# Cross-attention with group normalisation: whole-batch rounding and subtract, one chain of three GpSimd adds, and another order within a step

## The chip, the cores and the metric

The kernel runs on one core of one Trainium2 chip. The metric is the device time of one execution in microseconds (us). Engines are named as in the profile: PE is TensorE's matmul, PEld its weight load, DVE is VectorE, ACT is ScalarE, POOL is GpSimd, SP is SyncE, which issues the transfers of the loop.

## The reference

There are 32 batches. For each, `x` and `ctx` are 128 channels by 1024 positions, in float32.

```python
q = conv1x1(Wq, bq, ctx); k = conv1x1(Wk, bk, ctx); v = conv1x1(Wv, bv, x)   # 8 heads of 16 channels
scores = einsum('bhdl,bhel->bhde', q, k) / sqrt(128)       # channel by channel, within a head
attn = softmax(scores); out = einsum('bhde,bhel->bhdl', attn, v)
o = conv1x1(Wo, bo, out) + x
o_hat = (o - mean(o)) * rsqrt(var(o) + 1e-5)               # over all channels and positions of a batch
return o_hat * gn_w + gn_b
```

## The kernel before, in words

The scores need only the Gram matrix G = ctx·ctxᵀ (128x128) and the row sums s of ctx, and everything after the softmax is one matrix M with a bias, so that o = M·x. A batch thus goes through these pieces:

- **Gram.** ACT rounds ctx to a high part (`hl_sb[..., 0:C]`, line 340), DVE subtracts it from ctx to get the low part (`hl_sb[..., C:2C]`, line 432), PE multiplies the eight chunks into `g_ps` (`gram_products`, line 625). ACT copies the cross term (`b2_sb`, line 380), POOL adds up the low parts over the chunks (`lsuma`, `lsumb`, `lsum2`, `lsum`, lines 289 to 312), PE adds both into `g_ps`, and DVE writes `g_sb` and `s_sb` (lines 459, 460).
- **Scores.** PE makes `p_ps` from `g_sb` (`query_product`), DVE makes `p_sb` (line 477), PE makes `sc_ps` from `p_sb` and `sbk_sb` (lines 654, 655), DVE adds the mask and takes the smallest value of a row (`sc_sb`, `smin`, line 423).
- **Softmax and M.** ACT takes the exponential (line 335), DVE the reciprocal of the sums (`zinv`, line 443), ACT scales (line 352), PE multiplies (`softmax_product`), ACT copies (`r_sb`, line 363), PE makes `m_ps` in two products, DVE writes `m_sb` (`folded_matrix`, line 409).
- **Output.** PE makes `o_ps` in two halves of 512 columns (`products_of_x`), DVE takes statistics of each half (`bn`, lines 465 and 471), then `mv` and `mrow` (lines 502, 504). PE averages `mrow` over the channels (`mean`), DVE makes `dev` and `vrow` (lines 414, 416), PE averages `vrow` (`variance`), DVE makes `veps` (line 447), POOL makes `nshift`, `wshift` and `rstd` (lines 272 to 281), DVE makes `gain` and `shift` (lines 451, 453), and ACT writes the normalised batch to `out_sb` (line 371).

All matmuls are called through one helper, so all have line 535 in the trace and are told apart by their tiles.

The kernel is a software pipeline over the batches, written by hand. In step t every engine runs one fixed list of instructions, in which batch t is rounded, t-1 goes through the Gram products, t-2 through the scores, t-3 through softmax and M, t-4 through the output products and statistics, and t-5 is normalised. Each engine runs its list in order, step after step; engines are held together by semaphores alone, and an instruction whose semaphore isn't there holds up all that stands behind it on its engine. The two lists that matter most here are these, in a step of the kernel before:

- DVE: `dev`, `vrow` (batch t-5); `sc_sb`, `smin` (t-3); low part of the second half of ctx (t-1); `zinv`; `veps`; `g_sb`, `s_sb` (t-2); `bn` of the first half of o (t-4); `gain`, `shift` (t-5); `bn` of the second half; `p_sb`; `mv`, `mrow`; `m_sb`; low part of the first half of ctx (batch t).
- PE: first half of o; `variance`; the two additions into `g_ps`; second half of o; `query_product`; `softmax_product`; six Gram chunks; the two products of M; two Gram chunks; `mean`; the two products of `sc_ps`.

The lines on which the order rests:

```python
if has(t, 2):                     # PE, near the middle of its step
    query_product()               # waits for g_copied, which DVE's g_sb gives
...
    product(sc_ps, p_sb[:, :], wkT, stop=False)          # PE, the end of its step
    product(sc_ps, wqT[:, :], sbk_sb[:, :], start=False).then_inc(sc_ready, 1)
...
    dve.wait_ge(sc_ready, done)   # DVE, before sc_sb
```

Of the kernel before, what the change touches and what calls it, by code (L numbers as in the profile page):

```python
# [21 lines left out]
def xattn_groupnorm_kernel(nc, x, yT, weights, biases, columns, out):  # L22
# [27 lines left out]
    with ExitStack() as ctx:  # L50
# [338 lines left out]
        def _(dve):  # L389
            nc.vector.memset(onesn[:, :], 1.0 / E).then_inc(const_dve, 1)  # L390
# [10 lines left out]
            def step(t0, k):  # L401
# [9 lines left out]
                if has(t, 5):  # L411

                    dve.wait_ge(mu_ready, t - 4)
                    nc.vector.tensor_tensor(dev[:, h1:h1 + 1], mrow[:, h1:h1 + 1], mu_ps, ALU.subtract).then_inc(dev_ready, 1)  # L414
                    dve.wait_ge(dev_ready, t - 4)
                    nc.vector.tensor_scalar(vrow[:, h1:h1 + 1], dev[:, h1:h1 + 1], dev[:, h1:h1 + 1], mv[:, h1, 1:2],  # L416
                                            ALU.mult, ALU.add).then_inc(vrow_ready, 1)
# [9 lines left out]
                def rest_half(b, half):  # L427

                    ky = (k + b) % UNROLL
                    chunks = slice(half * HCH, (half + 1) * HCH)  # L430
                    dve.wait_ge(h_ready, (t + b) * 2 + 1 + half)
                    nc.vector.tensor_tensor(hl_sb[:, ky, chunks, C:2 * C], y_sb[:, ky, chunks, :],  # L432
                                            hl_sb[:, ky, chunks, 0:C].bitcast(F32), ALU.subtract).then_inc(l_ready, 1)
# [11 lines left out]
                def variance():  # L445
                    dve.wait_ge(var_ready, t - 4)
                    nc.vector.tensor_scalar(veps[:, h1:h1 + 1], var_ps, EPS, None, ALU.add).then_inc(veps_ready, 1)  # L447

                def affine():
                    dve.wait_ge(rstd_ready, t - 4)  # L450
                    nc.vector.tensor_scalar(gain[:, h1:h1 + 1], gn_w, rstd[:, h1:h1 + 1], None, ALU.mult)  # L451
                    dve.wait_ge(wshift_ready, t - 4)
                    nc.vector.tensor_scalar(shift[:, h1:h1 + 1], wshift[:, h1:h1 + 1], rstd[:, h1:h1 + 1], gn_b,  # L453
                                            ALU.mult, ALU.add).then_inc(affine_ready, 1)

                def gram():
# [4 lines left out]

                def statistics():

                    dve.wait_ge(o_ready, (t - 4) * 2 + 1)
                    nc.vector.bn_stats(bn[:, h, 0, :], o_ps[:, h, 0:HALF])  # L465
                    if has(t, 5) and not is_step(t, RUSH + 1):
                        affine()
                    if is_step(t, RUSH):
                        folded_matrix()
# [224 lines left out]
```

## Time and profile before

| | |
|---|---|
| time, median of 3 runs | 190.53 us (190.33 to 190.54) |
| the profiled execution: its own time | 190.41 us |
| its span, first to last instruction | 188.4 us |
| busy PE, DVE | 171.4 us, 162.1 us |
| busy ACT, POOL | 125.5 us, 125.7 us |
| mean granted TensorE clock | 0.968 of full |
| moved between HBM and the core | 50.8 MB, mean 270 GB/s |

Busy time of PE is modelled for overlapping matmuls and does not mean that it can go no faster. The 2.0 us between the profiled execution's time and its span lie before the first and after the last instruction. `sc_sb` is a good mark of a step, since it runs once in each from step 3 to step 34.

### The profile page before, as it was taken

The numbers are of one execution on the slowest core, as the hardware profiler recorded it, in microseconds if no ns is written. First come the engines' busy times: TensorE is split into PE (matmuls) and PEld (weight loads), VectorE is DVE, ScalarE is ACT, GpSimd is POOL, SyncE is SP. The second block draws the span as 40 slices with busy tenths as digits, with TensorE's granted clock in tenths as the row PEclk, the third lists the DMA queues.
The fourth block names the chain that finished last, engine by engine and source line by source line (L and its number), as shares of the span: only waits on it lengthen the run. The fifth ranks groups of instructions, "written<-read, shape, count | busy, mean of one in ns | idle before, by whom it ended". The sixth has DMA issues, their size and how long they took to land.

```text
span 188.4 us, 4194 instructions
## 1 busy us (share of the span) xinstructions
PE 171.4 (91%) x996; PEld 129.2 (69%) x996; DVE 162.1 (86%) x586; ACT 125.5 (67%) x290; POOL 125.7 (67%) x234
## 2 busy tenths in 40 slices
PE   7877999999999999999999999999999999998830
PEld 7767776767777777777677767776777767775420
DVE  1833899999899989998999989998999899977552
ACT  4433577787677877777777767876777777765321
POOL 3773577777777788877777777778777777762030
PEclk9985999999999999999999999999999999999995
DMA  6799377888878888888899787889888865622305
GB/s 211 264 418 381 94 277 250 322 325 320 310 284 296 303 288 297 317 303 318 304 324 342 291 289 273 317 296 305 291 313 315 321 229 223 221 100 88 148 23 203
DMA packets 14408, 50.82 MB, mean 270 GB/s; under 512 B 1728, under 2 KB 1856, under 8 KB 14400
## 3 DMA queue, kind: packets, MB, share of 16 engines
q1 hardware_dynamic: 13968, 50.34, 73.2%
q10 hardware_dynamic: 432, 0.40, 0.8%
q8 instruction: 3, 0.05, 0.1%
q14 instruction: 5, 0.04, 0.1%
HBM read 33.95 MB, written 16.78 MB: 269 GB/s over the span
## 4 chain that ended last, share of the span: by engine, by line
DVE 58%; issue 12%; POOL 7%; PE 6%; ACT 1%; POOLq 1%; DVEq 0%
DVE hl_sb L432 17%; DVE bn L471 10%; DVE bn L465 7%; POOL lsuma L312 4%; DVE mv L502 3%; DVE m_sb L409 3%; PE ps_ps L535 2%; DVE sc_sb L423 2%; DVE g_sb L459 2%; POOL rstd L281 2%; DVE shift L453 2%; DVE mrow L504 2%; PE st_ps L535 2%; DVE zinv L443 2%; DVE gain L451 2%
## 5 line engine op out<-in xcount | busy, mean ns | idle before, releaser
L535 PE MATMUL o_ps<-x_sb,m_sb 128*128 128x512 f32 x128 | 68.6, 618 | 0.4 <-DVE m_sb L409 0.4
L432 DVE TENSOR_TENSOR hl_sb<-y_sb,hl_sb 128x512 fp32r<-128x512 f32 x64 | 55.2, 863 | 2.3 <-ACT hl_sb L340 2.1
L535 PE MATMUL g_ps<-hl_sb 128*128 128x258 f32 x256 | 47.2, 308 | 0.0
L371 ACT ACTIVATE out_sb<-o_ps,shift,gain 128x1024 f32<-128x1024 f32 (+1 forms) x32 | 38.1, 1191 | 8.0 <-DVE shift L453 7.8
L340 ACT CAST hl_sb<-y_sb 128x512 fp32r<-128x512 f32 x64 | 39.1, 615 | 3.9 <-DMA y_sb<-in_ctx_dram 3.9
L304 POOL TENSOR_TENSOR lsum<-lsum 128x128 fp32r<-128x128 f32 x32 | 15.2, 474 | 33.1 <-DVE hl_sb L432 25.3
L535 PEld LDWEIGHTS g_ps<-hl_sb 128*128 128x128 f32 x256 | 35.7, 195 | 0.1
L312 POOL TENSOR_TENSOR lsuma<-hl_sb 128x256 f32<-128x256 f32 x32 | 27.4, 856 | 3.1 <-DVE hl_sb L432 3.1
L335 ACT ACTIVATE a_sb<-sc_sb,smin 128x128 f32<-128x128 f32 x32 | 12.9, 402 | 21.7 <-DVE smin L423 21.7
L296 POOL TENSOR_TENSOR lsum<-lsuma,lsumb 128x256 f32<-128x256 f32 x32 | 23.4, 730 | 4.3
L289 POOL TENSOR_TENSOR lsumb<-hl_sb 128x256 f32<-128x256 f32 x32 | 24.0, 750 | 1.4 <-DVE hl_sb L432 1.4
L535 PEld LDWEIGHTS ps_ps<-wqT,g_sb 128*128 128x128 f32 x64 | 10.4, 192 | 20.0 <-DVE g_sb L459 13.5
L535 PEld LDWEIGHTS st_ps<-vrow,onesn 128*128 128x128 f32 x64 | 12.0, 190 | 15.2 <-DVE vrow L416 8.0
L465 DVE BATCH_NORM_STATS2 bn<-o_ps 128x6 f32<-128x512 f32 x32 | 21.9, 685 | 0.2 <-PE o_ps L535 0.2
L471 DVE BATCH_NORM_STATS2 bn<-o_ps 128x6 f32<-128x512 f32 x32 | 21.9, 684 | 0.0
L272 POOL TENSOR_TENSOR nshift<-dev,mv 128x1 f32<-128x1 f32 x32 | 15.5, 483 | 8.7 <-DVE dev L414 8.7
L535 PEld LDWEIGHTS o_ps<-x_sb,m_sb 128*128 128x128 f32 x128 | 19.4, 192 | 0.8 <-DVE m_sb L409 0.5
L281 POOL TENSOR_TENSOR rstd<-veps,nhalf 128x1 f32<-128x1 f32 x32 | 17.5, 548 | 3.2 <-DVE veps L447 3.2
L535 PEld LDWEIGHTS st_ps<-mrow,onesn 128*128 128x128 f32 x64 | 9.5, 188 | 12.5 <-DVE mrow L504 12.5
L535 PE MATMUL st_ps<-mrow,onesn 128*128 128x1 f32 x64 | 12.1, 259 | 5.7 <-DVE mrow L504 4.6
L363 ACT COPY r_sb<-rm_ps 128x128 f32<-128x128 f32 x32 | 8.5, 266 | 12.8 <-PE rm_ps L535 12.8
L352 ACT ACTIVATE a_sb<-a_sb,zinv 128x128 f32<-128x128 f32 x32 | 12.8, 400 | 5.3 <-DVE zinv L443 5.2
(58 smaller groups left out, 315.3 us busy)
## 6 DMA issues: line engine op xcount, KB each, us to landing
y_sb<-in_ctx_dram SPq DMA_DIRECT2D x32, 512.0 KB, 3.9
x_sb<-in_x_dram SPq DMA_DIRECT2D x32, 512.0 KB, 4.9
out_dram<-out_sb SPq DMA_DIRECT2D x31, 512.0 KB, 3.9
out_dram<-out_sb SPq DMA_DIRECT2D x2, 256.0 KB, 2.2
w_in<-in_weights_dram ACTq DMA_DIRECT2D x1, 256.0 KB, 8.9
rows<-in_biases_dram ACTq DMA_DIRECT2D x1, 128.0 KB, 6.4
cols<-in_columns_dram ACTq DMA_DIRECT2D x1, 3.0 KB, 3.4
```

The costliest lines, as they stand in the source:

```text
L272: nc.gpsimd.tensor_tensor(nshift[:, h1:h1 + 1], dev[:, h1:h1 + 1], mv[:, h1, 0:1], ALU.subtract).then_inc(nshift_ready, 1)
L281: nc.gpsimd.tensor_tensor(rstd[:, h1:h1 + 1], veps[:, h1:h1 + 1], nhalf[:, :], ALU.pow).then_inc(rstd_ready, 1)
L289: nc.gpsimd.tensor_tensor(lsumb[:, :, :], low[:, 0:HCH // 2, :], low[:, HCH // 2:HCH, :], ALU.add).then_inc(lsumb_ready, 1)
L296: nc.gpsimd.tensor_tensor(lsum2[:, :, :], lsuma[:, :, :], lsumb[:, :, :], ALU.add).then_inc(lsum2_ready, 1)
L304: nc.gpsimd.tensor_tensor(lsum[:, h1, :], lsum2[:, 0, :], lsum2[:, 1, :], ALU.add).then_inc(lsum_ready, 1)
L312: nc.gpsimd.tensor_tensor(lsuma[:, :, :], low[:, 0:HCH // 2, :], low[:, HCH // 2:HCH, :], ALU.add).then_inc(lsuma_ready, 1)
L340: nc.scalar.copy(hl_sb[:, k, chunks, 0:C], y_sb[:, k, chunks, :]).then_inc(h_ready, 1)
L371: nc.scalar.activation(out_sb[:, ko, part], o_ps[:, h1, part], ACT.Identity, bias=shift[:, h1:h1 + 1], scale=gain[:, h1:h1 + 1]).then_inc( ...
L432: nc.vector.tensor_tensor(hl_sb[:, ky, chunks, C:2 * C], y_sb[:, ky, chunks, :], hl_sb[:, ky, chunks, 0:C].bitcast(F32), ALU.subtract).the ...
L465: nc.vector.bn_stats(bn[:, h, 0, :], o_ps[:, h, 0:HALF])
L471: nc.vector.bn_stats(bn[:, h, 1, :], o_ps[:, h, HALF:L]).then_inc(bn_done, 1)
L535: return nc.tensor.matmul(dst, lhsT, rhs, start=start, stop=stop, **more)
```

## The change

- **Rounding and subtract.** ACT rounds a whole batch of ctx (128x1024) at once, in the place of the first half; DVE makes the low part of the whole batch t-1 at once, right behind `sc_sb`. The semaphores count one per batch instead of two.
- **GpSimd.** The four adds of a batch (two of 256 columns from `hl_sb`, one of 256, one of 128) become three: `lsum4` (512 columns), `lsum2` (256), `lsum` (128). `nshift` and `wshift` leave GpSimd, and `rstd` stays, now first in its step.
- **Mean and variance.** `onesn` holds -1/128. PE's `mean` stands between the products of M and the last two Gram chunks. DVE's `dev` and `vrow` run at the end of the same step instead of at the start of the next, and between them stands a new instruction that makes `wshift` there.
- **Gain and shift.** Both move from DVE to ACT, behind the scaling by `zinv` and ahead of `sbk_sb` and `r_sb`.
- **DVE's order.** In a step it is now: `sc_sb`, `smin`; low part of the whole batch t-1; `zinv`; `veps`; `bn` of the first half; `g_sb`, `s_sb`; `bn` of the second half; `mv`, `mrow`; `p_sb`; `m_sb`; `dev`, `wshift`, `vrow`. PE's list is otherwise as before.

The first steps and the last three have the same moves, with the exceptions for `RUSH` (step 34) simplified: in step 35 the mean no longer stands behind the first half of o.

```diff
 POOL
-                    pool.wait_ge(dev_ready, t - 4)
-                    nc.gpsimd.tensor_tensor(nshift[:, h1:h1 + 1], dev[:, h1:h1 + 1], mv[:, h1, 0:1],
-                                            ALU.subtract).then_inc(nshift_ready, 1)
...
-                    nc.gpsimd.tensor_tensor(wshift[:, h1:h1 + 1], nshift[:, h1:h1 + 1], gn_w,
-                                            ALU.mult).then_inc(wshift_ready, 1)
                     pool.wait_ge(veps_ready, t - 4)
                     nc.gpsimd.tensor_tensor(rstd[:, h1:h1 + 1], veps[:, h1:h1 + 1], nhalf[:, :], ALU.pow).then_inc(rstd_ready, 1)
...
-                    nc.gpsimd.tensor_tensor(lsumb[:, :, :], low[:, 0:HCH // 2, :], low[:, HCH // 2:HCH, :],
-                                            ALU.add).then_inc(lsumb_ready, 1)
+                    nc.gpsimd.tensor_tensor(lsum4[:, :, :], low[:, 0:HCH, :], low[:, HCH:CH, :],
+                                            ALU.add).then_inc(lsum4_ready, 1)
...
-                if has(t, 0):
...
-                    nc.gpsimd.tensor_tensor(lsuma[:, :, :], low[:, 0:HCH // 2, :], low[:, HCH // 2:HCH, :],
-                                            ALU.add).then_inc(lsuma_ready, 1)
 ACT
-                    round_half(0)
+                    nc.scalar.copy(hl_sb[:, k, :, 0:C], y_sb[:, k, :, :]).then_inc(h_ready, 1)
                 if has(t, 3):
                     act.wait_ge(zinv_ready, t - 2)
                     nc.scalar.mul(a_sb[:, :], a_sb[:, :], zinv[:, h1:h1 + 1]).then_inc(a_ready, 1)
+                if has(t, 5):
+                    act.wait_ge(rstd_ready, t - 4)
+                    nc.scalar.mul(gain[:, h1:h1 + 1], gn_w, rstd[:, h1:h1 + 1])
+                    nc.scalar.activation(shift[:, h1:h1 + 1], wshift[:, h1:h1 + 1], ACT.Identity,
+                                         bias=gn_b, scale=rstd[:, h1:h1 + 1]).then_inc(affine_ready, 1)
 DVE
-                if has(t, 1):
-                    rest_half(-1, 1)
+                if has(t, 1):
+                    ky = (k - 1) % UNROLL
+                    dve.wait_ge(h_ready, t)
+                    nc.vector.tensor_tensor(hl_sb[:, ky, :, C:2 * C], y_sb[:, ky, :, :],
+                                            hl_sb[:, ky, :, 0:C].bitcast(F32), ALU.subtract).then_inc(l_ready, 1)
...
-                if has(t, 2):
-                    gram()
-                if has(t, 4):
-                    statistics()
+                if has(t, 4):
+                    dve.wait_ge(o_ready, (t - 4) * 2 + 1)
+                    nc.vector.bn_stats(bn[:, h, 0, :], o_ps[:, h, 0:HALF])
...
+                if has(t, 2):
                     dve.wait_ge(g_ready, t - 1)
                     nc.vector.tensor_tensor(g_sb[:, :], g_ps[:, 0:C], b2_sb[:, :].bitcast(F32), ALU.add).then_inc(g_copied, 1)
                     nc.vector.tensor_copy(s_sb[:, :], s_ps).then_inc(s_copied, 1)
...
-                if has(t, 0):
-                    rest_half(0, 0)
+                if has(t, 4):
+                    dve.wait_ge(mu_ready, t - 3)
+                    nc.vector.tensor_tensor(dev[:, h:h + 1], mrow[:, h:h + 1], mu_ps, ALU.add).then_inc(dev_ready, 1)
...
+                    nc.vector.scalar_tensor_tensor(out=wshift[:, h:h + 1], in0=mu_ps, scalar=m_sb[:, h, E:E + 1],
+                                                   in1=gn_w, op0=ALU.add, op1=ALU.mult)
+                    dve.wait_ge(dev_ready, t - 3)
+                    nc.vector.tensor_scalar(vrow[:, h:h + 1], dev[:, h:h + 1], dev[:, h:h + 1], mv[:, h, 1:2],
+                                            ALU.mult, ALU.add).then_inc(vrow_ready, 1)
 PE
                     product(m_ps[:, E:E + 1], r_sb[:, :], bv).then_inc(m_ready, 1)
+                if has(t, 4):
+                    mean()
                 if has(t, 1):
                     gram_products(range(GRAM_BEFORE_M, CH)).then_inc(hl_ready, 1)
...
-                if has(t, 4) and not is_step(t, RUSH):
-                    mean(-4)
```

## Rows read from the trace of the kernel before

**Rows 1.** The page: busy time by engine, and the chain that ended last.

```profile
PE 171.4 (91%) x996; PEld 129.2 (69%) x996; DVE 162.1 (86%) x586; ACT 125.5 (67%) x290; POOL 125.7 (67%) x234
...
DVE 58%; issue 12%; POOL 7%; PE 6%; ACT 1%; POOLq 1%; DVEq 0%
```

**Rows 2.** Timeline, one steady step: start, duration, engine, instruction, [idle before, releaser].

```profile
96.87 0.29 DVE L423 CUSTOM_DVE_ANT_0 sc_sb<-ps_ps,k 128x128 f32<-128x128 f32 x1
...
97.03 0.73 POOL L312 TENSOR_TENSOR lsuma<-hl_sb 128x256 f32<-128x256 f32 x1
...
97.17 1.14 DVE L432 TENSOR_TENSOR hl_sb<-y_sb,hl_sb 128x512 fp32r<-128x512 f32 x1
...
98.23 0.15 DVE L443 RECIPROCAL zinv<-zsum 128x1 f32<-128x1 f32 x1
...
98.36 0.28 DVE L459 TENSOR_TENSOR g_sb<-g_ps,b_sb 128x128 f32<-128x128 f32 x1
...
98.57 0.55 POOL L281 TENSOR_TENSOR rstd<-veps,nhalf 128x1 f32<-128x1 f32 x1
98.62 0.69 DVE L465 BATCH_NORM_STATS2 bn<-o_ps 128x6 f32<-128x512 f32 x1
98.69 0.30 PEld L535 LDWEIGHTS ps_ps<-wqT,g_sb 128*128 128x128 f32 x2 [0.63 <-DVE g_sb L459]
...
99.01 0.39 PE L535 MATMUL rm_ps<-w_in,a_sb 128*128 128x128 f32 x2
...
99.22 0.19 DVE L451 TENSOR_SCALAR gain<-cols,rstd 128x1 f32<-128x1 f32 x1
...
99.44 0.27 ACT L363 COPY r_sb<-rm_ps 128x128 f32<-128x128 f32 x1 [0.30 <-PE rm_ps L535]
...
100.33 0.49 PE L535 MATMUL g_ps<-hl_sb 128*128 128x258 f32 x2
...
100.87 0.30 PEld L535 LDWEIGHTS st_ps<-mrow,onesn 128*128 128x128 f32 x2 [0.27 <-DVE mrow L504]
...
101.42 0.39 PE L535 MATMUL ps_ps<-sbk_sb,wqT 128*128 128x128 f32 x2
...
101.96 0.29 DVE L423 CUSTOM_DVE_ANT_0 sc_sb<-ps_ps,k 128x128 f32<-128x128 f32 x1
```

**Rows 3.** Timeline of DVE in every fourth step, where the subtract meets no GpSimd add.

```profile
86.50 0.29 DVE L423 CUSTOM_DVE_ANT_0 sc_sb<-ps_ps,k 128x128 f32<-128x128 f32 x1
...
86.72 0.69 DVE L432 TENSOR_TENSOR hl_sb<-y_sb,hl_sb 128x512 fp32r<-128x512 f32 x1
87.36 0.16 DVE L443 RECIPROCAL zinv<-zsum 128x1 f32<-128x1 f32 x1
```

**Rows 4.** Timeline of PE in an early step, where the mean came without a wait.

```profile
23.36 0.49 PE L535 MATMUL g_ps<-hl_sb 128*128 128x258 f32 x2
...
24.14 0.39 PE L535 MATMUL ps_ps<-sbk_sb,wqT 128*128 128x128 f32 x2
```

**Rows 5.** Groups by line and shape, GpSimd's adds: busy us, mean ns, idle before.

```profile
L289 POOL TENSOR_TENSOR lsumb<-hl_sb 128x256 f32<-128x256 f32 x32 | 24.0, 750 | 1.4 <-DVE hl_sb L432 1.4
...
L304 POOL TENSOR_TENSOR lsum<-lsum 128x128 fp32r<-128x128 f32 x32 | 15.2, 474 | 33.1 <-DVE hl_sb L432 25.3 <-issue 7.6
```

**Rows 6.** Timelines: `sc_sb` of steps 3, 4, 6 and 33.

```profile
14.21 0.29 DVE L423 CUSTOM_DVE_ANT_0 sc_sb<-ps_ps,k 128x128 f32<-128x128 f32 x1 [1.09 <-PE ps_ps L535]
...
20.03 0.29 DVE L423 CUSTOM_DVE_ANT_0 sc_sb<-ps_ps,k 128x128 f32<-128x128 f32 x1 [0.46 <-PE ps_ps L535]
...
29.91 0.29 DVE L423 CUSTOM_DVE_ANT_0 sc_sb<-ps_ps,k 128x128 f32<-128x128 f32 x1
...
168.72 0.29 DVE L423 CUSTOM_DVE_ANT_0 sc_sb<-ps_ps,k 128x128 f32<-128x128 f32 x1 [0.20 <-PE ps_ps L535]
```

**Rows 7.** Windows of the start: busy PE, PEld, DVE, ACT, POOL, then clock, DMA share, GB/s.

```profile
9.40:14.10 4.70, 3.33 (x21) 3.17 (x21) 1.81 (x6) 1.80 (x4) 3.32 (x6) 0.85 1.03 418
14.10:18.80 4.70, 3.50 (x17) 3.41 (x17) 1.75 (x8) 1.86 (x6) 1.76 (x3) 0.50 1.01 383
```

More of the change, by code:

```diff
@@ L285, in step @@
-                    pool.wait_ge(l_ready, t * 2)
+                    low = hl_sb[:, (k - 1) % UNROLL, :, C:2 * C].bitcast(F32)
+                    pool.wait_ge(l_ready, t)
                     if exists(t, 2):
                         pool.wait_ge(lsum2_ready, t - 1)
-                    nc.gpsimd.tensor_tensor(lsumb[:, :, :], low[:, 0:HCH // 2, :], low[:, HCH // 2:HCH, :],
-                                            ALU.add).then_inc(lsumb_ready, 1)
-                    pool.wait_ge(lsuma_ready, t)
@@ L380, in step @@
                     nc.scalar.copy(b2_sb[:, :], g_ps[:, C:2 * C]).then_inc(b2_copied, 1)
-                if has(t, 0) and not ahead:
-                    round_half(1)
             pipeline(act, step, first=3 * UNROLL)
@@ L409, in folded_matrix @@
                     nc.vector.tensor_tensor(m_sb[:, h1, :], m_ps, ident[:, :], ALU.add).then_inc(m_copied, 1)
[L411 to L417, printed above, removed]
                 if has(t, 3):
@@ L425, in step, with variance @@
                                                    accum_out=smin[:, h1:h1 + 1]).then_inc(smin_ready, 1)
[L427 to L433, printed above, removed]
+                def variance():
+                    dve.wait_ge(var_ready, t - 4)
+                    nc.vector.tensor_scalar(veps[:, h1:h1 + 1], var_ps, -1.0, EPS, ALU.mult, ALU.add).then_inc(veps_ready, 1)
+                if has(t, 5) and is_step(t, RUSH):
+                    variance()
                 if has(t, 1):
-                    rest_half(-1, 1)
+                    ky = (k - 1) % UNROLL
+                    dve.wait_ge(h_ready, t)
+                    nc.vector.tensor_tensor(hl_sb[:, ky, :, C:2 * C], y_sb[:, ky, :, :],
+                                            hl_sb[:, ky, :, 0:C].bitcast(F32), ALU.subtract).then_inc(l_ready, 1)
                 if is_step(t, 2):
@@ L440, in step @@
                     nc.vector.tensor_scalar(wqT[:, :], w_in[:, 0, :], -SCALE, None, ALU.mult).then_inc(const_dve, 1)
-                def inverse_sums():
+                if has(t, 3):
                     dve.wait_ge(exp_done, t - 2)
                     nc.vector.reciprocal(zinv[:, h1:h1 + 1], zsum[:, h1:h1 + 1]).then_inc(zinv_ready, 1)
[L445 to L456, printed above, removed]
+                if has(t, 5) and not is_step(t, RUSH) and not is_step(t, RUSH + 1):
+                    variance()
+                if has(t, 4):
+                    dve.wait_ge(o_ready, (t - 4) * 2 + 1)
+                    nc.vector.bn_stats(bn[:, h, 0, :], o_ps[:, h, 0:HALF])
+                if is_step(t, RUSH + 1):
+                    variance()
+                if has(t, 2):
                     dve.wait_ge(g_ready, t - 1)
@@ L460, in gram @@
                     nc.vector.tensor_copy(s_sb[:, :], s_ps).then_inc(s_copied, 1)
[L462 to L469, printed above, removed]
+                if is_step(t, RUSH):
+                    folded_matrix()
+                if has(t, 4):
+                    done = value(t - 3)
                     dve.wait_ge(o_ready, (t - 3) * 2)
                     nc.vector.bn_stats(bn[:, h, 1, :], o_ps[:, h, HALF:L]).then_inc(bn_done, 1)
[L473 to L499 removed]
                     dve.wait_ge(c_loaded, 16 * N_CONST)
@@ L579, in softmax_product, with mean @@
                     product(r_ps, a_sb[:, :], woT).then_inc(r_ready, 1)
-                def mean(b):
-                    pe.wait_ge(mrow_ready, t + b + 1)
-                    if exists(t, 1 - b):
-                        pe.wait_ge(veps_ready, t + b)
-                    row = (h + b) % 2
-                    product(mu_ps, onesn[:, :], mrow[:, row:row + 1]).then_inc(mu_ready, 1)
+                def mean():
+                    pe.wait_ge(mrow_ready, t - 3)
+                    if exists(t, 5):
+                        pe.wait_ge(veps_ready, t - 4)
+                    product(mu_ps, onesn[:, :], mrow[:, h:h + 1]).then_inc(mu_ready, 1)
                 if has(t, 5) and is_step(t, RUSH):
@@ L598, in step @@
                     products_of_x(0)
-                if is_step(t, RUSH + 1):
-                    mean(-5)
-                elif has(t, 5) and not is_step(t, RUSH):
+                if has(t, 5) and not is_step(t, RUSH):
                     variance()
@@ L643, in step @@
                     product(m_ps[:, E:E + 1], r_sb[:, :], bv).then_inc(m_ready, 1)
+                if has(t, 4):
+                    mean()
                 if has(t, 1):
```

67 lines of the change are left out of this document (16 added, 51 removed).

## The prediction

> **What bounds the kernel now.** I read the page first: DVE and PE are both near full, and the chain that ended last runs mostly on DVE [rows 1]. That suggests that a microsecond taken from DVE is a microsecond won. It is only half the story, so I looked next at the timeline of one steady step, side by side for DVE and PE [rows 2], and followed who hands what to whom. Each engine works its list in order, and two hand-overs join the lists into a ring. `sc_sb`, the first of the big instructions of DVE's step, starts 0.15 us after PE's last product of the step before ends (101.42 + 0.39 = 101.81, against 101.96). And PE's `query_product` can't load before DVE's `g_sb` ends (98.64; the load starts at 98.69, after an idle weight port released by `g_sb`). Everything that PE does from there to its `sc_ps` products stands in order behind `query_product`. So a step can't be shorter than DVE's stretch from `sc_sb` to the end of `g_sb` (98.64 - 96.87 = 1.77), plus PE's stretch from there to the end of `sc_ps` (101.81 - 98.64 = 3.17), plus 0.15: together 5.09, which is exactly the distance of the two `sc_sb` in rows 2. Within PE's stretch lies a wait of 0.27 for `mrow`, which is DVE work behind `g_sb`. The ring and DVE's own load are thus both tight: DVE is without a real pause, and what DVE has after `g_sb` reaches PE through `mrow`.
>
> Over the whole run the step is a little longer: 27 steps from `sc_sb` at 29.91 to the one at 168.72 [rows 6] take 138.81, or 5.14 each.
>
> **The change part by part, for a steady step.** I place it against `sc_sb` = 0.
>
> DVE up to `g_sb`. The low part is now one subtract of 1024 columns. In the kernel before, the subtract of 512 in this place took 1.14, because it met POOL's add (97.03 to 97.76, [rows 2]): what is left after 97.76 is 0.55, the time of 512 columns. Where it met none it took 0.69, started 0.22 after `sc_sb` and gave way to `zinv` 0.64 later [rows 3]. The extra 512 columns cost 0.53 (a `bn` of 512 columns against 128 columns of `g_sb`: (0.69 - 0.28)/384 = 1.07 ns a column, 0.55 for 512; 0.60 with a start of its own). I take 0.53, so `zinv` starts at 0.22 + 0.64 + 0.53 = 1.39, against 1.36 before (98.23 - 96.87). So the bigger subtract costs nothing in this stretch, *if* POOL is idle during it. It is: POOL's chain starts behind `rstd`, about 1.70 to 2.25; an add of 512 columns is (750 - 474)/128 = 2.16 ns a column, so 0.75 + 0.55 = 1.30; then 0.75 and 0.47 [rows 5]; with gaps it ends at about 5.0, and the next subtract starts at 5.6.
>
> From `zinv` to `g_sb` were 0.13 us (98.23 to 98.36). Now `bn` of the first half stands between: its slot is 0.60 (98.62 to 99.22). Its data are long there. So `g_sb` starts at 1.39 + 0.13 + 0.60 = 2.12 and ends at 2.40, where it was 1.77. That is +0.63 on the ring.
>
> The Trainium skill ("SBUF — State Buffer", section "SBUF: two separate sides") says that the port pair that VectorE and GpSimd share is an exclusive lock, held for a whole instruction by a VectorE instruction with two SBUF inputs or by GpSimd. The trace agrees: 1.14 against 0.69 [rows 2, 3]. By that rule alone the change looks like a gain on VectorE of some 0.45 us a step, for the subtract then meets nobody.
>
> PE from `g_sb` to `sc_ps`. The weight load follows 0.05 after `g_sb`; 0.32 later `softmax_product` runs (98.69 to 99.01); 1.32 later come the last two Gram chunks (99.01 to 100.33). From there to the end of `sc_ps` with a mean that did not wait: 24.14 + 0.39 - 23.36 = 1.17 [rows 4], against 1.48 before. The mean's new place, two products earlier, doesn't change the sum, and it will not wait: DVE has `mrow` done at about 3.6, PE reaches the mean at 4.1. PE's stretch is 0.05 + 0.32 + 1.32 + 1.17 = 2.86, where it was 3.17: -0.31, the wait for `mrow` that goes.
>
> The step: 2.40 + 2.86 + 0.15 = **5.41**. PE now stands idle about 0.6 before `query_product`; DVE stands idle before `sc_sb`.
>
> What DVE saves buys nothing. It loses the collision (0.45), one start of a subtract (0.06), and `gain` and `shift` (99.22 to about 99.52, 0.30), and gains `wshift` (not in the trace; between 0.06 and 0.25, the slots of one-column and of 128-column instructions; I take 0.12). That brings it from 5.09 to about 4.4. All of it lies behind `g_sb` or, for the subtract, is used up ahead of it. Its end: `m_sb` waits for PE's second product of M (about 4.2), `dev` for the mean (4.5), and `vrow` ends near 5.0, 0.4 before the next `sc_sb`; so those waits stay off the ring.
>
> ACT. The round of 1024 columns follows the exponential and ends at about 1.9, half a step before it is needed by the next step. `gain` waits for `rstd` (ready at 2.3: `veps` at 1.46, then 0.55 on POOL [rows 2]). `gain`, `shift` and `sbk_sb` then end at about 3.1. Behind them is `r_sb`, whose product is ready at 3.2; PE wants it after six Gram chunks, at 3.8, and it takes 0.27 [rows 2]. So ACT's insertion costs nothing, with 0.3 of cover. The output instruction of 1.2 us ends near 4.7 and PE wants its buffer at 5.1.
>
> Transfers. SP's load of ctx waits for the whole low part, as it did for the second half, at the same place; at 5.41 us a step the demand falls. Cost 0.
>
> **The sum.** 27 steps from step 6 to 33: 27 x 5.41 = 146.1 against 138.8: +7.3. Steps 4 to 6 (20.03 to 29.91, 9.88 for two): 10.82, +0.9. Step 3 to 4: no `bn` yet, but the whole subtract stands before `g_sb`: +0.5. The first Gram matrix waits for the weights' transfer either way: 0. Step 33 has no subtract, and its mean no longer waits: -0.3. The tail: in step 34 the mean of batch 30 stands ahead of the first half of o of batch 31 (+1.3 on PE), but DVE no longer makes `gain` and `shift` before `mv` of batch 31; I find +0.1. Sum +8.5. On the profiled execution's own 190.41 this is 198.9; the median of the runs, 190.53, gives 199.0.
>
> **Rivals.**
> 1. *DVE alone is the bound* (for: 58% of the chain and no pause [rows 1]). Then its savings count, and PE's load, at most 5.09 - 0.27 = 4.82, is the next bound: (4.82 - 5.14) x 29 = -9, so **181**. Against it: `query_product` waits for `g_sb` by the code, and the row shows that wait. It decides if PE's stretch were 0.3 shorter than I read. 0.07. A ring that comes out at 5.14, no change: 0.03; a ring just below, 186 to 190: 0.03.
> 2. *ACT becomes part of the ring.* If `rstd` comes over 0.3 later than 2.3 or ACT's one-column instructions are as long as the 128-column ones, `r_sb` comes late for M, at 0.1 to 0.3 a step: **202 to 207**. A collision of POOL's chain with the subtract (if it ends after 5.6) would give as much. 0.12.
> 3. *The granted clock.* At the start it fell to 0.50, which is the 1.2 GHz level, after a stretch in which PE was busy for 3.33 of 4.70 us [rows 7]. PE will be busy for 4.8 of 5.4 in the steady steps, so I expect full clock there. But step 3 gets another 0.5 of idleness; if the low clock lasts one step longer, PE's 4.8 us of work in it takes up to twice as long: +2 to +4, **201 to 203**. 0.10. The Trainium skill ("TensorE: Matmul & The Clock Gate", section "What's actually happening") says that the throttled state is the default and activity releases it, which is what rows 7 show in small.
> 4. The forecast itself, 196 to 201.5: 0.65.
>
> The range: the terms unsure by about 0.1 a step give 2.8 either way; with the lower part of rivals 2 and 3 it is 195.5 to 203.5. A difference under 0.2% can't be told from none here. Faster 0.09, same 0.03, slower 0.88.
>
> **What would show it.** `sc_sb` every 5.4 us; the subtract at 1.2 us with POOL idle; `zinv` 1.4 after `sc_sb` and `g_sb` 2.1 after it; PE's weight load for `query_product` idle by about 0.6, released by `g_sb`; no wait for `mrow` before the mean; DVE waiting on PE before `sc_sb`, for some 0.4 a step, and its busy share down to about 80%. I am wrong if PE's wait before `query_product` is near zero, or if a step shows a new wait for `r_sb` or `rstd`.

## The result, and the profile after

The changed kernel takes 197.92 us (median of 4 runs, 196.82 to 199.13); the kernel before took 190.43 beside it. The ratio is 1.0405, with a 95% interval of 1.0331 to 1.0479: slower, by about 4%. The forecast was 199.0. Ratios, here and below, are of the executions in the faster of two states alone; the medians are of all.

The page of the changed kernel, busy time by engine and the chain that ended last, answers to [rows 1]:

```profile
PE 169.0 (86%) x996; PEld 125.8 (64%) x996; DVE 145.6 (74%) x522; ACT 137.5 (70%) x322; POOL 98.2 (50%) x138
...
PE 39%; DVE 27%; issue 19%; POOL 6%; DMA 5%; DVEq 1%; POOLq 1%; ACT 0%; ACTq 0%
```

DVE has lost 16.5 us of work and POOL 27.5, and the span grew from 188.4 to 195.6. No engine is above 86% of the span. In the steady part, 28.2 to 170 us, PE was busy for 131.01 of 141.80 us (92%, before 98%) and DVE for 116.31 (82%, before 96%). So neither is full any more; the time is set by who waits for whom, and the chain runs back and forth between PE and DVE. The list of waits names the pair (waiting instruction <- what it waited for: us in total, times, longest):

```profile
PEld ps_ps L479 <- DVE g_sb L419: 30.7, 25, 1.7
...
DVE sc_sb L384 <- PE ps_ps L479: 15.0, 32, 1.3
...
PE ps_ps L479 <- DVE g_sb L419: 14.5, 31, 1.6
...
ACT gain L326 <- POOL rstd L267: 11.3, 31, 4.1
```

In the step shown below the weight load (PEld) stands idle for 1.23 us before `query_product` and the matmuls for 0.40; in [rows 2] the weight load had 0.63 and the matmuls no wait. So the row of the matmuls tells better what PE lost.

Timeline of the changed kernel, one steady step, to be laid beside [rows 2]:

```profile
100.60 0.29 DVE L384 CUSTOM_DVE_ANT_0 sc_sb<-ps_ps,k 128x128 f32<-128x128 f32 x1 [0.43 <-PE ps_ps L479]
...
100.82 1.22 DVE L398 TENSOR_TENSOR hl_sb<-y_sb,hl_sb 128x1024 fp32r<-128x1024 f32 x1
...
101.96 0.15 DVE L407 RECIPROCAL zinv<-zsum 128x1 f32<-128x1 f32 x1
...
102.09 0.69 DVE L413 BATCH_NORM_STATS2 bn<-o_ps 128x6 f32<-128x512 f32 x1
...
102.69 0.27 DVE L419 TENSOR_TENSOR g_sb<-g_ps,b_sb 128x128 f32<-128x128 f32 x1
...
102.77 1.28 POOL L275 TENSOR_TENSOR lsum<-hl_sb 128x512 f32<-128x512 f32 x1
102.83 0.29 ACT L326 ACTIVATE gain<-cols,rstd 128x1 f32<-128x1 f32 x1 [0.16 <-POOL rstd L267]
...
103.02 0.49 PE L479 MATMUL ps_ps<-wqT,g_sb 128*128 128x128 f32 x2 [0.40 <-DVE g_sb L419]
...
103.34 0.39 PE L479 MATMUL rm_ps<-w_in,a_sb 128*128 128x128 f32 x2
...
103.77 0.27 ACT L339 COPY r_sb<-rm_ps 128x128 f32<-128x128 f32 x1
...
103.99 0.21 DVE L432 TENSOR_SCALAR mrow<-mv,m_sb 128x1 f32<-128x1 f32 x1
...
104.18 0.31 PEld L479 LDWEIGHTS rm_ps<-r_sb,w_in 128*128 128x128 f32 x2
...
104.63 0.30 PEld L479 LDWEIGHTS st_ps<-mrow,onesn 128*128 128x128 f32 x2
...
104.83 0.29 DVE L377 TENSOR_TENSOR m_sb<-rm_ps,ident 128x129 f32<-128x129 f32 x1 [0.38 <-PE rm_ps L479]
...
104.88 0.48 PE L479 MATMUL g_ps<-hl_sb 128*128 128x258 f32 x2
...
105.42 0.39 PE L479 MATMUL ps_ps<-sbk_sb,wqT 128*128 128x128 f32 x2
...
105.95 0.29 DVE L384 CUSTOM_DVE_ANT_0 sc_sb<-ps_ps,k 128x128 f32<-128x128 f32 x1 [0.43 <-PE ps_ps L479]
```

Read it as a ring. From `sc_sb` to the end of `g_sb` are 102.96 - 100.60 = 2.36 us; from there to the end of PE's `sc_ps` 105.81 - 102.96 = 2.85; then 0.14 to the next `sc_sb`: 5.35 in all. The subtract of 1024 columns lets `zinv` start 1.36 after `sc_sb`, as it was before with 512 columns and a collision. All the growth of the first stretch is the 0.60 of `bn`, which now stands between `veps` and `g_sb`. The weight load of `mean` (104.63) shows no wait, as `mrow` had ended at 104.20; before it had 0.27. Both engines of the ring now have pauses, DVE 0.43 before `sc_sb` (and 0.38 before `m_sb`), PE 0.40 before `query_product`.

`sc_sb` of steps 4, 6 and 33 in the changed kernel, which answer to [rows 6]:

```profile
20.16 0.29 DVE L384 CUSTOM_DVE_ANT_0 sc_sb<-ps_ps,k 128x128 f32<-128x128 f32 x1 [1.31 <-PE ps_ps L479]
...
30.80 0.29 DVE L384 CUSTOM_DVE_ANT_0 sc_sb<-ps_ps,k 128x128 f32<-128x128 f32 x1 [0.43 <-PE ps_ps L479]
...
175.76 0.29 DVE L384 CUSTOM_DVE_ANT_0 sc_sb<-ps_ps,k 128x128 f32<-128x128 f32 x1 [0.44 <-PE ps_ps L479]
```

The 27 steps between the last two take 144.96, or 5.37 each (three of 5.35 and one of 5.43 for each turn of the loop), against 138.81 before. That is +6.15 of the +7.2 by which the span grew. Steps 4 to 6 give +0.76, step 3 to 4 +0.33, step 33 to 34 -0.18, the tail +0.34, and the start up to step 3 -0.20.

### The profile page after: what moved, and what is told of

Same layout as the page of the kernel before. It is cut to its first block, busy times and chain, and to the rows that moved or that the text cites. A ratio compares the mean times of both kernels' runs of the same rounds, so it can differ in the third digit from the quotient of the medians.

```text
span 195.6 us, 3989 instructions
## 1 busy us (share of the span) xinstructions
PE 169.0 (86%) x996; PEld 125.8 (64%) x996; DVE 145.6 (74%) x522; ACT 137.5 (70%) x322; POOL 98.2 (50%) x138
## 4 chain that ended last, share of the span: by engine, by line
PE 39%; DVE 27%; issue 19%; POOL 6%; DMA 5%; DVEq 1%; POOLq 1%; ACT 0%; ACTq 0%
PE g_ps L479 15%; PE ps_ps L479 13%; DVE hl_sb L398 10%; DVE bn L413 8%; PE rm_ps L479 8%; DMA w_in<-in_weights_dram 5%; PE st_ps L479 3%; DVE g_sb L419 3%; DVE sc_sb L384 3%; POOL lsum L275 3%; DVE zinv L407 2%; POOL lsum L281 1%; POOL rstd L267 1%; POOL lsum L287 1%; DVE veps L390 1%
## 5 line engine op out<-in xcount | busy, mean ns | idle before, releaser
L275 POOL TENSOR_TENSOR lsum<-hl_sb 128x512 f32<-128x512 f32 x32 | 40.9, 1278 | 10.3 <-DVE hl_sb L398 10.3
L398 DVE TENSOR_TENSOR hl_sb<-y_sb,hl_sb 128x1024 fp32r<-128x1024 f32 x32 | 39.1, 1221 | 2.6 <-ACT hl_sb L318 2.6
L318 ACT CAST hl_sb<-y_sb 128x1024 fp32r<-128x1024 f32 x32 | 33.1, 1033 | 3.8 <-DMA y_sb<-in_ctx_dram 3.8
L479 PEld LDWEIGHTS ps_ps<-wqT,g_sb 128*128 128x128 f32 x64 | 9.5, 188 | 39.5 <-DVE g_sb L419 30.7
L479 PE MATMUL ps_ps<-wqT,g_sb 128*128 128x128 f32 x64 | 15.6, 325 | 14.5 <-DVE g_sb L419 14.5
L281 POOL TENSOR_TENSOR lsum<-lsum 128x256 f32<-128x256 f32 x32 | 23.4, 732 | 2.5
L384 DVE CUSTOM_DVE_ANT_0 sc_sb<-ps_ps,k 128x128 f32<-128x128 f32 x32 | 9.3, 292 | 15.0 <-PE ps_ps L479 15.0
L377 DVE TENSOR_TENSOR m_sb<-rm_ps,ident 128x129 f32<-128x129 f32 x32 | 9.4, 294 | 14.6 <-PE rm_ps L479 14.5
L352 ACT CAST b_sb<-g_ps 128x128 fp32r<-128x128 f32 x32 | 8.5, 266 | 13.3 <-PE g_ps L479 13.3
L326 ACT ACTIVATE gain<-cols,rstd 128x1 f32<-128x1 f32 x32 | 9.4, 295 | 11.3 <-POOL rstd L267 11.3
```

What stands on the lines that cost most here:

```text
L275: nc.gpsimd.tensor_tensor(lsum4[:, :, :], low[:, 0:HCH, :], low[:, HCH:CH, :], ALU.add).then_inc(lsum4_ready, 1)
L281: nc.gpsimd.tensor_tensor(lsum2[:, :, :], lsum4[:, 0:HCH // 2, :], lsum4[:, HCH // 2:HCH, :], ALU.add).then_inc(lsum2_ready, 1)
L318: nc.scalar.copy(hl_sb[:, k, :, 0:C], y_sb[:, k, :, :]).then_inc(h_ready, 1)
L384: nc.vector.tensor_tensor_reduce(out=sc_sb[:, :], in0=sc_ps, in1=k0[:, :], scale=1.0, scalar=3e38, op0=ALU.add, op1=ALU.min, accum_out=smi ...
L398: nc.vector.tensor_tensor(hl_sb[:, ky, :, C:2 * C], y_sb[:, ky, :, :], hl_sb[:, ky, :, 0:C].bitcast(F32), ALU.subtract).then_inc(l_ready, 1)
L479: return nc.tensor.matmul(dst, lhsT, rhs, start=start, stop=stop, **more)
```

## The experiments

The measure I trust most is the step, (`sc_sb` of step 33 less that of step 6)/27 in the profile, because executions of one kernel differ at their start. Times are medians; ratios are to the kernel before, measured beside each.

| kernel | step, us | time, us | ratio (95%) |
|---|---|---|---|
| before | 5.14 | 190.53 | |
| changed | 5.37 | 197.92 | 1.0405 (1.0331 to 1.0479) |
| 1 changed, `g_sb` first | 5.10 | 190.29 | 0.9993 (0.9934 to 1.0052) |
| 2 before, first `bn` ahead of `g_sb` | 5.39 | 196.39 | 1.0377 (1.0292 to 1.0461) |
| 3 changed, `gain` and `shift` on DVE | 5.37 | 199.58 | 1.0540 (1.0451 to 1.0629) |
| 4 changed, 0.33 us more ahead of `g_sb` | 5.70 | 208.37 | 1.0972 (1.0873 to 1.1071) |
| 5 changed, the same at the step's end | 5.37 | 197.82 | 1.056 (1.0479 to 1.0641) |
| 6 as 1, `sbk_sb` ahead of `gain` | 4.97 | 186.57 | none |
| 7 as 6, `mean` behind the Gram chunks | 4.87 | 183.69 | 0.9744 (0.9692 to 0.9795) |
| 8 as 1, `gain`/`shift` on DVE, `mean` late | 5.08 | 189.30 | 1.0046 (1.0015 to 1.0077) |
| 9 changed, idle products in step 3 | 5.37 | 196.67 | 1.0415 (1.0373 to 1.0457) |
| 10 as 7, idle products in step 3 | 4.87 | 182.30 | 0.9639 (0.9586 to 0.9691) |
| 11 as 7, again | 4.87 | 182.96 | 0.9655 (0.9601 to 0.9709) |

**1. Undo the one move in the changed kernel.**

```diff
 DVE, changed kernel
+                if has(t, 2):
+                    dve.wait_ge(g_ready, t - 1)
+                    nc.vector.tensor_tensor(g_sb[:, :], g_ps[:, 0:C], b2_sb[:, :].bitcast(F32), ALU.add).then_inc(g_copied, 1)
+                    nc.vector.tensor_copy(s_sb[:, :], s_ps).then_inc(s_copied, 1)
                 if has(t, 4):
                     dve.wait_ge(o_ready, (t - 4) * 2 + 1)
                     nc.vector.bn_stats(bn[:, h, 0, :], o_ps[:, h, 0:HALF])
-                if has(t, 2):
-                    dve.wait_ge(g_ready, t - 1)
-                    nc.vector.tensor_tensor(g_sb[:, :], g_ps[:, 0:C], b2_sb[:, :].bitcast(F32), ALU.add).then_inc(g_copied, 1)
-                    nc.vector.tensor_copy(s_sb[:, :], s_ps).then_inc(s_copied, 1)
```

> The changed kernel with g_sb and s_sb ahead of the first bn on DVE, nothing else. Theory (the ring sc_sb, g_sb, query_product, sc_ps sets the step): g_sb ends at about 1.76 us after sc_sb instead of 2.36, so the wait of PE before query_product goes. PE then comes early enough to wait for mrow (done 3.60 after sc_sb, mean reached at about 3.4): a step of about 4.95 instead of 5.37, time 185 to 187. Rival (the cause is ACT's gain and shift, or the whole-batch subtract): the place of one statistics instruction among DVE's changes nothing, the time stays at 197 to 199.

The step fell to 5.10 and the time to that of the kernel before. So the place of `g_sb` was the loss, but the gain was 0.27 a step where I expected 0.42, and the time stayed above the expected 185 to 187. The timeline of this kernel shows why:

```profile
92.39 0.28 DVE L413 TENSOR_TENSOR g_sb<-g_ps,b_sb 128x128 f32<-128x128 f32 x1
...
93.14 0.30 ACT L326 ACTIVATE gain<-cols,rstd 128x1 f32<-128x1 f32 x1 [0.16 <-POOL rstd L267]
...
93.33 0.37 ACT L327 ACTIVATE shift<-wshift,cols,rstd 128x1 f32<-128x1 f32 x1
...
93.61 0.39 ACT L335 ACTIVATE sbk_sb<-rows,s_sb 128x128 f32<-128x128 f32 x1
93.91 0.24 ACT L339 COPY r_sb<-rm_ps 128x128 f32<-128x128 f32 x1
...
94.20 0.30 PEld L479 LDWEIGHTS rm_ps<-r_sb,w_in 128*128 128x128 f32 x2 [0.17 <-ACT r_sb L339]
```

`g_sb` is ready 0.60 sooner (its end comes 1.76 after `sc_sb`, against 2.36), and PE now arrives at the products of M before `r_sb` is there. ACT copies `r_sb` only after `gain`, `shift` and `sbk_sb`, and `gain` waits for POOL's `rstd`. This was rival 2 of the prediction, hidden in the changed kernel by the later `g_sb`. Run 6 tests it.

**2. Do the one move alone, in the kernel before.**

```diff
 DVE, kernel before
                 def statistics():
-                    dve.wait_ge(o_ready, (t - 4) * 2 + 1)
-                    nc.vector.bn_stats(bn[:, h, 0, :], o_ps[:, h, 0:HALF])
...
+                if has(t, 4):
+                    dve.wait_ge(o_ready, (t - 4) * 2 + 1)
+                    nc.vector.bn_stats(bn[:, h, 0, :], o_ps[:, h, 0:HALF])
                 if has(t, 2):
                     gram()
```

> The kernel before with only this of the change: the first bn ahead of g_sb and s_sb on DVE. Theory: the ring grows by the 0.60 us of bn and loses the wait for mrow of 0.27, so a step of about 5.42 instead of 5.14 and a time of 197 to 200: this one move gives the whole loss. Rival: the loss comes from the other parts of the change, and the time stays within 1 us of 190.5.

The step is 5.39, and the time 196.39, a little below the expected 197 to 200. In the step this one move costs as much as the whole change (+0.25 against +0.23), and in the time nearly as much. The rest of the change, on which DVE and POOL save 44 us of busy time, shows no gain beside it (5.37 against 5.39). A small part of this kernel's step is DVE's own list: in three of four steady steps `sc_sb` starts 0.20 after PE's `sc_ps` ends, where it is 0.14 in the changed kernel. PE's wait appears in this kernel's timeline too, though DVE has all its old work:

```profile
101.27 0.27 DVE L459 TENSOR_TENSOR g_sb<-g_ps,b_sb 128x128 f32<-128x128 f32 x1
...
101.59 0.49 PE L536 MATMUL ps_ps<-wqT,g_sb 128*128 128x128 f32 x2 [0.51 <-DVE g_sb L459]
...
103.41 0.29 DVE L409 TENSOR_TENSOR m_sb<-rm_ps,ident 128x129 f32<-128x129 f32 x1 [0.28 <-PE rm_ps L536]
```

**3. Take back ACT's part.** `gain` and `shift` go back to DVE, between the second `bn` and `mv`.

```diff
 ACT
-                if has(t, 5):
-                    act.wait_ge(rstd_ready, t - 4)
-                    nc.scalar.mul(gain[:, h1:h1 + 1], gn_w, rstd[:, h1:h1 + 1])
-                    nc.scalar.activation(shift[:, h1:h1 + 1], wshift[:, h1:h1 + 1], ACT.Identity,
-                                         bias=gn_b, scale=rstd[:, h1:h1 + 1]).then_inc(affine_ready, 1)
 DVE
                     nc.vector.bn_stats(bn[:, h, 1, :], o_ps[:, h, HALF:L]).then_inc(bn_done, 1)
+                if has(t, 5):
+                    dve.wait_ge(rstd_ready, t - 4)
+                    nc.vector.tensor_scalar(gain[:, h1:h1 + 1], gn_w, rstd[:, h1:h1 + 1], None, ALU.mult)
+                    nc.vector.tensor_scalar(shift[:, h1:h1 + 1], wshift[:, h1:h1 + 1], rstd[:, h1:h1 + 1], gn_b,
+                                            ALU.mult, ALU.add).then_inc(affine_ready, 1)
+                if has(t, 4):
```

> The changed kernel with gain and shift back on DVE, behind the second bn. Theory: 0.30 us more on DVE lies behind g_sb and inside its idle time, and ACT's load of two instructions was covered: no change in the step (5.37), time 197 to 199. Rival (ACT's two instructions hold up r_sb or the output): the step falls by 0.1 to 0.3, time 189 to 195. Rival (DVE's load is what counts): plus 0.3 a step, 206.

The step is 5.37, unchanged: two instructions on either engine are off the ring, as the theory says. The time is 0.6 us above the expected range. In the profile the surplus over the changed kernel lies outside the steps: `sc_sb` of step 6 comes at 32.24 instead of 30.80, and the tail behind `sc_sb` of step 34 is 16.1 instead of 15.3. The start had the low clock for longer (0.50 and 0.58 between 14.1 and 23.5 us, where the changed kernel had 0.76 and 0.88). Whether this edit has a part in that is not settled.

**4 and 5. The same cost in two places.** One more statistics instruction of 256 columns a step, which nobody reads.

```diff
 DVE, run 4
                     nc.vector.bn_stats(bn[:, h, 0, :], o_ps[:, h, 0:HALF])
+                    nc.vector.bn_stats(extra[:, :], o_ps[:, h, 0:HALF // 2])
```

```diff
 DVE, run 5
                                             ALU.mult, ALU.add).then_inc(vrow_ready, 1)
+                    nc.vector.bn_stats(extra[:, :], o_ps[:, h, 0:HALF // 2])
```

> The changed kernel with one more statistics instruction of 256 columns a step on DVE, between the first bn and g_sb; nobody reads what it writes. Its slot is about 0.33 us. Theory: all of it lands on the ring, 30 x 0.33 = 10 us, time 207 to 209. Rival (DVE has 25% idle and PE is the bound): less than 2 us.

> The changed kernel with the same additional statistics instruction of 256 columns (0.33 us), now at the end of DVE's step, behind vrow. Theory: DVE waits there for PE anyway, 0.43 us before each sc_sb, so the instruction is hidden: step 5.37, time as the changed kernel within 1.5 us (196 to 199.5). Rival (any DVE work costs): 207.

Ahead of `g_sb` it lengthens each step from 5.37 to 5.70: all of its 0.33 slot (103.37 to 103.70 in that kernel's timeline), and PE's wait before `query_product` grows by the same, from 0.40 to 0.73. At the end of the step it costs nothing, 5.37. Its timeline shows it in what was the wait for `sc_ps`:

```profile
104.37 0.27 DVE L453 TENSOR_SCALAR vrow<-dev,mv 128x1 f32<-128x1 f32 x1
104.55 0.42 DVE L455 BATCH_NORM_STATS2 extra<-o_ps 128x6 f32<-128x256 f32 x1
105.07 0.29 DVE L385 CUSTOM_DVE_ANT_0 sc_sb<-ps_ps,k 128x128 f32<-128x128 f32 x1
```

This is the cleanest reading of the case: the same instruction on the same engine costs everything or nothing, by where it stands. (The ratio of run 5 is high because the kernel before was faster beside it, 188.36; the step, which repeats within 0.01, shows no cost.)

**6. Free `r_sb` in the order of run 1.**

```diff
 ACT, on top of run 1
+                if has(t, 2):
+                    if is_step(t, 2):
+                        act.wait_ge(c_loaded, 16 * N_CONST)
+                    act.wait_ge(s_copied, t - 1)
+                    nc.scalar.mul(sbk_sb[:, :], bkB, s_sb[:, :]).then_inc(sbk_ready, 1)
                 if has(t, 5):
                     act.wait_ge(rstd_ready, t - 4)
...
-                if has(t, 2):
-                    if is_step(t, 2):
-                        act.wait_ge(c_loaded, 16 * N_CONST)
-                    act.wait_ge(s_copied, t - 1)
-                    nc.scalar.mul(sbk_sb[:, :], bkB, s_sb[:, :]).then_inc(sbk_ready, 1)
```

> The changed kernel with g_sb ahead of the first bn and, on ACT, sbk_sb ahead of gain and shift. With g_sb first alone the step came to 5.10 instead of 4.95, because PE waited 0.17 us for r_sb, which stood behind rstd, gain, shift and sbk_sb on ACT. Theory: with sbk_sb in ACT's wait for rstd, r_sb comes 0.24 us sooner and the wait goes; the step falls to 4.93 to 4.97, time 184.5 to 187. Rival (r_sb was not what held it): 5.10, 189 to 190.

`sbk_sb` now fills ACT's wait for `rstd`, PE no longer waits for `r_sb`, and the step is 4.97, as expected. No ratio could be taken for it (its seven executions spread from 183.30 to 188.52), and the reading rests on the step.

**7. Put `mean` back.**

```diff
 PE, on top of run 6
-                if has(t, 4):
-                    mean()
                 if has(t, 1):
                     gram_products(range(GRAM_BEFORE_M, CH)).then_inc(hl_ready, 1)
...
+                if has(t, 4):
+                    mean()
```

> As the run with sbk_sb ahead of gain and shift, and PE's mean back behind the last two Gram chunks. Theory: PE then doesn't meet mrow too early either, and is the bound by its own work of about 4.73: a step of 4.73 to 4.82, time 180 to 183. Rival (the mean's place is free, as DVE is held up by the mean at its end instead): as the run before it, 4.95.

The step is 4.87 and the time 183.69, both a little above what was expected (4.73 to 4.82, and 180 to 183): PE's own work was counted too low. It is faster than both kernels, by 2.6% against the one before. The mean's early place costs 0.10 once the ring is short. In run 6 its weight load starts 0.34 after the one before it, where the next follows in 0.22, and it starts 0.05 after the end of `mrow` (104.20):

```profile
103.91 0.30 PEld L479 LDWEIGHTS rm_ps<-cols,r_sb 128*128 128x128 f32 x2
...
103.99 0.21 DVE L432 TENSOR_SCALAR mrow<-mv,m_sb 128x1 f32<-128x1 f32 x1
...
104.25 0.30 PEld L479 LDWEIGHTS st_ps<-mrow,onesn 128*128 128x128 f32 x2
...
104.47 0.30 PEld L479 LDWEIGHTS g_ps<-hl_sb 128*128 128x128 f32 x2
```

In the changed kernel `mrow` is there 0.43 before the load, so the early place should cost nothing there; no run puts it back in that kernel alone. In run 7's timeline the chain `g_sb`, `r_sb`, `mean`, `sc_sb` is now nearly without waits:

```profile
97.63 0.29 DVE L384 CUSTOM_DVE_ANT_0 sc_sb<-ps_ps,k 128x128 f32<-128x128 f32 x1 [0.31 <-PE ps_ps L479]
...
99.11 0.28 DVE L413 TENSOR_TENSOR g_sb<-g_ps,b_sb 128x128 f32<-128x128 f32 x1
...
100.41 0.24 ACT L339 COPY r_sb<-rm_ps 128x128 f32<-128x128 f32 x1
...
101.38 0.31 PEld L479 LDWEIGHTS st_ps<-mrow,onesn 128*128 128x128 f32 x2
...
102.48 0.29 DVE L384 CUSTOM_DVE_ANT_0 sc_sb<-ps_ps,k 128x128 f32<-128x128 f32 x1 [0.16 <-PE ps_ps L479]
```

Its page says who sets the time now, PE (busy for 139.57 of 141.80 us in the steady part), with DVE 17 us below the kernel before:

```profile
PE 168.3 (92%) x996; PEld 128.8 (71%) x996; DVE 145.1 (80%) x522; ACT 131.1 (72%) x322; POOL 98.5 (54%) x138
...
PE 70%; issue 13%; POOL 6%; DMA 5%; DVE 3%; POOLq 1%; ACT 1%; ACTq 0%; DVEq 0%
```

**8. Another way to free `r_sb`.** On top of run 1: `mean` late, and `gain` and `shift` on DVE between the two `bn` (in step 35 behind the second).

```diff
 DVE
                     nc.vector.bn_stats(bn[:, h, 0, :], o_ps[:, h, 0:HALF])
+                if has(t, 5) and not is_step(t, RUSH + 1):
+                    dve.wait_ge(rstd_ready, t - 4)
+                    nc.vector.tensor_scalar(gain[:, h1:h1 + 1], gn_w, rstd[:, h1:h1 + 1], None, ALU.mult)
+                    nc.vector.tensor_scalar(shift[:, h1:h1 + 1], wshift[:, h1:h1 + 1], rstd[:, h1:h1 + 1], gn_b,
+                                            ALU.mult, ALU.add).then_inc(affine_ready, 1)
...
                     nc.vector.bn_stats(bn[:, h, 1, :], o_ps[:, h, HALF:L]).then_inc(bn_done, 1)
```

> The changed kernel with g_sb ahead of the first bn, gain and shift on DVE between the two bn as in the kernel before, and the mean behind the last two Gram chunks. Theory: r_sb is free of rstd, DVE's load is 4.4 + 0.3 = 4.7 and PE's 4.73, but mrow comes 0.3 later: a step of 4.80 to 4.90, time 181.5 to 185. Rival (DVE as the bound again): 5.1, 189.

It came out at 5.08, the number of the rival, but not for its reason, for DVE still has a pause before `sc_sb`:

```profile
101.17 0.28 DVE L407 TENSOR_TENSOR g_sb<-g_ps,b_sb 128x128 f32<-128x128 f32 x1
...
103.36 0.21 DVE L437 TENSOR_SCALAR mrow<-mv,m_sb 128x1 f32<-128x1 f32 x1
103.49 0.34 DVE L443 SCALAR_TENSOR_TENSOR p_sb<-bqB,s_sb,ps_ps 128x128 f32<-128x128 f32 x1
...
103.89 0.49 PE L484 MATMUL ps_ps<-w_in,p_sb 128*128 128x128 f32 x2
...
104.75 0.29 DVE L378 CUSTOM_DVE_ANT_0 sc_sb<-ps_ps,k 128x128 f32<-128x128 f32 x1 [0.19 <-PE ps_ps L484]
```

`p_sb` ends at 103.83 and PE's first product of `sc_ps` starts at 103.89: the ring has moved from PE's list to DVE's. From `g_sb` it now runs over both `bn`, `gain`, `shift`, `mv`, `mrow` and `p_sb`. By this reading each of these should count; no run takes one of them away.

**9 to 11. The start.** The granted clock between 9 and 24 us differs from execution to execution.

```diff
 PE, ahead of the second half of o, step 3 alone
+                if is_step(t, 3):
+                    keep_busy(2 * FILL)
```

> The changed kernel with four idle products of 128 columns added on PE in step 3 alone, in its 1.6 us wait for g_sb; nobody reads them. Theory: executions differ at the start by the granted clock (0.50 to 1.00 between 9 and 24 us), and work in that gap keeps it at 2.4 GHz: the slowest executions fall away, median 1 to 2 us lower (196 to 197), and the step stays at 5.37. Rival (the gap has no part in the clock): as the changed kernel.

> The fastest so far (g_sb first, sbk_sb ahead of gain, mean late) with the same four idle products in step 3. Theory: step 4.87 as without, start without the low clock: 181.5 to 183 instead of 183.7. Rival: no effect, 183 to 184.5.

> The fastest so far once more, beside the run with the added products: 183 to 184.5 us, step 4.87.

Two windows of the start (busy time by engine, then granted clock, DMA share, GB/s), of the changed kernel and then of run 9:

```profile
14.10:18.80 4.70, 3.09 (x17) 2.97 (x17) 2.27 (x8) 2.29 (x6) 2.47 (x3) 0.76 0.95 355
```

```profile
14.10:18.80 4.70, 4.09 (x31) 3.59 (x30) 2.49 (x11) 2.56 (x7) 2.47 (x3) 1.00 0.99 375
```

The same window of run 8, which has no added products, and then of run 10, which has them:

```profile
14.10:18.80 4.70, 3.11 (x23) 2.81 (x23) 2.50 (x11) 2.56 (x7) 2.47 (x3) 1.00 0.98 375
```

```profile
14.10:18.80 4.70, 3.91 (x31) 3.65 (x29) 2.11 (x7) 2.56 (x7) 1.97 (x2) 0.92 0.70 270
```

In run 9 the clock stayed at 1.00, 2.4 GHz, from 9.4 to 23.5 us, and step 3 to 4 took 4.61 us instead of 6.15. But run 8 had 1.00 and 4.61 there too, without the products, and run 10 with them had 0.72 between 9.4 and 14.1 us, where run 11 had 0.77. So the profiles do not show that the products keep the clock up. Run 9's six executions lie within 1.0 us (196.35 to 197.38), where the four of the changed kernel spread over 2.3. But the ratio to the kernel before is the same (1.0415 against 1.0405), and for runs 10 and 11 the intervals overlap; run 11, without the products, had step 3 to 4 in 4.61 as well. The times of runs 9 and 10 (196.67, 182.30) fall in the expected ranges and that of run 11 (182.96) just below its own, but that says nothing about the products. Their effect on the clock and on the time stays open.

## Why the prediction was right

- **What bounds the kernel.** Right. The ring `sc_sb`, `g_sb`, `query_product`, `sc_ps` sets the step. Runs 4 and 5 show it most directly, and runs 1 and 2 show the move of `g_sb` as the cause from both sides.
- **The stretch on DVE.** Forecast 2.40, measured 2.36. `zinv` came at 1.36 (forecast 1.39), and the slot of `bn` was 0.60. POOL was idle during the subtract as forecast (its first add starts at 102.77, the subtract ends at 102.04), which took 1.22 us. The lock of the shared port pair, as the Trainium skill has it ("SBUF — State Buffer", section "SBUF: two separate sides"), agrees: with no GpSimd add beside it the subtract took 1.22 us in every steady step. The gain of 0.45 that the rule alone would give was used up by the other 512 columns (1.22 against 0.69), and the 0.60 of `bn` came on top. One thing in [rows 3] has to be put right: in that step of the kernel before, the two did meet, but the subtract came first (86.72) and the add waited, which is why it took 1.26 instead of 0.73. So the 0.45 was to be had in three steps of four:

```profile
86.74 1.26 POOL L312 TENSOR_TENSOR lsuma<-hl_sb 128x256 f32<-128x256 f32 x1
```

- **The stretch on PE.** Forecast 2.86, measured 2.85. The wait for `mrow` of 0.27 [rows 2] went, as forecast.
- **The sum.** Forecast +8.5, measured +7.2 in the span of the profiled executions. The term of the steady steps was mis-sized by 0.04 a step (+7.3 forecast, +6.15 measured), the start by 0.5 (+1.4 against +0.9); step 33 and the tail came out 0.1 and 0.2 above their terms. The step was added up for the one that is shown, which took 5.35 where 5.41 was forecast, and then used as the mean of 27, which was 5.37. In the kernel before the mean had been 0.05 above the step shown (5.14 against 5.09), and the sum has no term for that; here it was only 0.02, so little hung on it.
- **DVE's savings.** Right that they buy nothing. Its load of about 4.4 us a step was right: in the steady part its busy share is 82%, beside the 80 that I wrote. The page's 74% takes in the start and the tail. PE's pause before `query_product` was 0.40 in the row of the matmuls. I had written 0.6 for the weight load, whose own row shows 1.23; that row had 0.63 already in the kernel before [rows 2], and it is the growth that is 0.60.
- **Rival 1**, DVE as the bound, fell: DVE lost 16.5 us and the kernel became slower.
- **Rival 2**, ACT in the ring, did not happen in the changed kernel, where `r_sb` ended at 104.04 and PE loaded it at 104.18. My cover of 0.3 was 0.14. ACT's side was right: `sbk_sb` ended 3.10 after `sc_sb` (forecast 3.1) and `r_sb` at 3.44. PE's side was wrong: I had PE reach `r_sb` at 3.8, and it did so at 3.58. The kernel before would have told it, for there this load starts 1.21 after the end of `g_sb`, and 2.40 + 1.21 is 3.61:

```profile
99.85 0.31 PEld L535 LDWEIGHTS rm_ps<-r_sb,w_in 128*128 128x128 f32 x2
```

  With `g_sb` 0.60 sooner in run 1 the ring ran into ACT's list, which is why that run came out at 5.10 and not at 4.95.
- **Rival 3**, the clock. In the steady part it stayed at 1.00. At the start it was low for part of the time, in the changed kernel as in the one before; the four runs' mean clocks order them (0.982, 0.979, 0.972, 0.956 for 196.82, 197.39, 198.45, 199.13). That step 3's longer idle stretch lowered it is not shown: the kernel before had 0.50 between 14.1 and 18.8 us [rows 7] and the changed kernel 0.76.

## What to carry to other kernels

In a hand-written pipeline with in-order engines, find the ring first: for each pair of engines, the hand-over that one waits for and the work that stands between it and the hand-over back. Only what stands on that ring costs time; so put whatever feeds the other engine ahead of work that nobody waits for, and ask of each moved instruction which side of the hand-over it lands on. When a ring is cut short, look for the next one before claiming the gain: here it took three moves (`g_sb` ahead of `bn`, `sbk_sb` ahead of `gain`, `mean` late) to turn savings that were worth nothing into 2.6% to 3.5%.

## What the hardware showed that I had not expected

- ACT's rounding of 1024 columns takes 1.03 us, against 0.615 for 512 columns in the kernel before: the second 512 columns cost 0.42. The whole-batch form is cheaper by 0.20 a batch.
- One-column instructions are dearer on ACT than on DVE: `gain` 0.30 against 0.20, `shift` 0.37 against 0.26.
- The start varies more than the steady part. Step 3 to 4 took 6.15 us in the changed kernel and 6.55 in run 3; it took 5.44 in run 7 and 4.61 in run 11, which are the same kernel; the clock there was between 0.50 and 1.00. The mean step of runs 7 and 11 agrees within 0.01 us.
